# Nine columns instead of ten in the per-block list of edges outside the grid

## The chip, the cores and the metric

The kernel runs on one core of a Trainium2 chip. The metric is the device time of one execution in microseconds (us). TensorE is PE in the tables, VectorE DVE, ScalarE ACT, GpSimd POOL and SyncE SP.

## What is computed

Four graph layers run one after the other on 6,250 nodes with 64 features and 206,250 directed edges, sorted by destination. Each layer adds its result to x and normalizes. Cut to what matters (`w1`, `w2` are edge weights, `ea` the 32 features of an edge):

```
edges: 100000 random (s, d), both ways, and 6250 loops; sorted by dst
layer 0: relu(segment_sum(w1 * (x @ W_low)[src], dst)), the same with w2, W_high; attention of three branches
layer 1: segment_sum / max / mean(ea, by src) -> 2-layer MLP
layer 2: sum over k of segment_sum(gw_k(deg[src], deg[dst]) * (x @ g)_k[src], dst) / deg
layer 3: segment_sum(relu(W1 @ [x[src], x[dst], ea]) @ W2.T, dst) -> GRU cell
after each: x = layernorm(x + layer)
```

## The kernel before

The edges are cut into `NBK` = 51 blocks of `BE` = 4,096, read as 32 chunks of 128. Since they are sorted by destination, the destinations of a block lie within some 128 neighbouring nodes. A block has two stores in DRAM. One is a **grid** with one cell for each source node (49 x 128 cells): an edge may lie there if, counting chunk by chunk up to and with its own, it is the only edge of the block with its source, and its destination is under 128 above the block's first. All other edges go into the **list** of the block, in order. The list is cut into pieces of `SR = P * SC` slots, with `SC` columns of 128; a block has room for `NR` = 4 such pieces, and slots with no edge hold a fill row (source 6250, destination 6272, weights 0).

`placing` (L223) counts, decides for each edge, and scatters the rows. It ends with the number of rounds, from the longest list (`k.n_sec`, in slots):

```
incl[0] = max over blocks of n_sec
rounds  = 1 + (incl[0] > SR) + (incl[0] > 2 * SR) + (incl[0] > 3 * SR)     # L558 to L566
```

`k.counts_i[0]` holds it, `n_rounds` (L597) loads it into a register of each engine, and it is the count of the outer loop of `over_rounds` (L570) and `over_triples` (L583), each of which runs over all 51 blocks for every round:

```
with eng.Fori(0, rounds) as r:
    with eng.Fori(0, thirds // 2) as i: ...body(n, m, b, j, r)
```

Four stages run in this loop, and each round works on piece `r` of every block's list:

- **layer-0 sums** (`layer0_rest`, L613): POOL gathers the source rows of a piece, one indirect DMA for each column (L672), DVE weighs them and builds one-hot masks (L729, L741, L743), PE sums into 160 destinations (L704) and counts degrees (L708, three columns at a time). SP loads the pieces and, in the same body, writes zeros and far marks for later stages (L654, L655). The grid's part of layer 0 was done in `placing`.
- **layer-1 scatter** (`layer1_scatter`, L1012): sorts the list's rows by source; POOL scatters one column with each indirect DMA (L1091), to places from DVE (L1207); DVE ranks within a column (L1183).
- **layer-2 edges** (`layer2_edges`, L1638): each body does the grid (294 matmuls at L1712, masks at L1761) and the piece of the list (gathers at L1692, matmuls at L1725).
- **layer-3 edges** (`layer3_edges`, L2020): again the grid (L2145, L2149, L2163, L2166) and the piece (two gathers for a column, L2113 and L2116; masks L2307, matmuls L2214).

In the second and later rounds of layers 2 and 3 the grid's relative destinations come from the far marks (-128), so that its masks are all zero, but its instructions are the same. A block takes one of three buffers (`j`), semaphores set the order, and each engine follows its own stream. The order around the change is as written; nothing plans it.

Of the kernel before, what the change touches and what calls it, by code (L numbers as in the profile page):

```python
# [4 lines left out]
P = 128  # L5
CB = 32
BE = P * CB
SC = 10
SR = P * SC
NR = 4  # L10
SUB = 7
D = 64
F = 32
# [14 lines left out]
ACT = mybir.ActivationFunctionType  # L28
# [51 lines left out]
def make(nc, ctx):  # L80
    def sb(name, shape, dt=fp32):
        return ctx.enter_context(nc.sbuf_tensor(name, shape, dt))

    def ps(name, shape, dt=fp32):
        return ctx.enter_context(nc.psum_tensor(name, shape, dt))

    def sem(name):
        return nc.alloc_semaphore(name)

    return sb, ps, sem  # L90
# [132 lines left out]
def placing(nc, z, k, a):  # L223
    NT, NBK, HC = z.NT, z.NBK, CB // 2
    BK = 8
    with ExitStack() as ctx:
# [48 lines left out]
        gv = a["pay_d"][0:z.grid_rows, :].rearrange("(b l s) w -> b l (s w)", l=P, s=NT)  # L275
        sv = a["pay_d"][z.grid_rows:z.grid_rows + z.sec_rows, :].rearrange("(b p r) w -> b p (r w)", p=P, r=NR * SC)
        fg = a["fill"][0:z.cells, :].rearrange("(l s) w -> l (s w)", l=P)
# [292 lines left out]
def over_rounds(eng, z, k, body):  # L570
    thirds = z.NBK // 3
    rounds = n_rounds(eng, k)
    with eng.Fori(0, rounds) as r:
        with eng.Fori(0, thirds // 2) as i:
            for h in range(2):
                for j in range(3):
                    body(r * z.NBK + i * 6 + (h * 3 + j), r * thirds + i * 2 + h, i * 6 + (h * 3 + j), j, r)
        for m in range(thirds - thirds % 2, thirds):
            for j in range(3):
                body(r * z.NBK + (m * 3 + j), r * thirds + m, m * 3 + j, j, r)  # L580
# [28 lines left out]
def sec_view(z, a):  # L609
    return a["pay_d"][z.grid_rows:z.grid_rows + z.sec_rows, :].rearrange("(k p c) w -> k p (c w)", p=P, c=SC)  # L610


def layer0_rest(nc, z, k, a):  # L613
    NBK = z.NBK
    with ExitStack() as ctx:
        sb, ps, sem = make(nc, ctx)
        row = [sb(f"r0_row{j}", [P, SC, RW]) for j in range(3)]
        xs = [sb(f"r0_x{j}", [P, SC, D]) for j in range(3)]
        val = [sb(f"r0_val{j}", [P, SC, 2 * D]) for j in range(3)]
        onehot = [sb(f"r0_onehot{j}", [P, SC, WS]) for j in range(3)]  # L620
# [391 lines left out]
def layer1_scatter(nc, z, k, a):  # L1012
    NT = z.NT
    with ExitStack() as ctx:
# [11 lines left out]
        lo_hot = sb("s_lo_hot", [P, SC * P])  # L1026
# [8 lines left out]
        turned = ps("s_turned", [P, 2, 1024], bf16)  # L1035
# [11 lines left out]
        with nc.Block() as block:  # L1047
            @block.sync
            def _(sp):
                sp.wait_ge(nothing_set, 1)  # L1050

                pairs = scan_pairs(sp, z, k)

                def clear(j):
                    for q in range(4):
                        sp.dma_start(quarter(a["sorted_d"], z, pairs, q, j), nothing[:, :]).then_inc(cleared, 16)

                for j in range(3):
                    clear(j)
                with sp.Fori(0, pairs) as i:  # L1060
                    clear(i * 2 + 3)
                    clear(i * 2 + 4)

                def load(at_row, m, j):
                    sp.wait_ge(rows_out[j], m * (SC * 16) + 16)
                    sp.sem_inc(k.sync_steps, 1)
                    sp.dma_start(row[j][:, :, :].rearrange("p c w -> p (c w)"),
                                 sv[bass.ds(at_row, 1)].rearrange("k p w -> (k p) w")).then_inc(row_in[j], 16)

                def body(n, m, b, j, r):  # L1070
                    load(b * NR + r, m, j)

                over_rounds(sp, z, k, body)
                rounds = n_rounds(sp, k)
                load(0, rounds * (z.NBK // 3), 0)
# [24 lines left out]
            @block.scalar  # L1100
            def _(act):
                sc = nc.scalar

                def spread(n, j):
                    act.wait_ge(keys_ready, n + 1)
                    sc.activation(keys[:, :, :], key[j][:, :].unsqueeze(2).to_broadcast([P, SC, P]), ACT.Copy).then_inc(bc_in, 1)

                def copies(n):
                    act.wait_ge(turned_ready, n + 1)
                    sc.activation(lo_hot[:, 0:8 * P], turned[:, 0, :], ACT.Copy).then_inc(lo_hot_ready, 1)  # L1110
                    sc.activation(lo_hot[:, 8 * P:SC * P], turned[:, 1, 0:2 * P], ACT.Copy).then_inc(lo_hot_ready, 1)

                def body(n, m, b, j, r):
                    spread(n + 1, (j + 1) % 3)
                    copies(n + 1)

                spread(0, 0)
                copies(0)
                over_rounds(act, z, k, body)
# [900 lines left out]
def layer3_edges(nc, z, k, a):  # L2020
# [6 lines left out]
    with ExitStack() as ctx:  # L2027
# [16 lines left out]
        ea_s = sb("m_ea_s", [P, 3 * P])  # L2044
# [7 lines left out]
        pre_s = ps("m_pre_s", [P, 2, 512])  # L2052
# [13 lines left out]
        with nc.Block() as block:  # L2066
# [154 lines left out]
            @block.scalar  # L2221
            def _(act):
                sc = nc.scalar

                def copies(n, u):
                    act.wait_ge(turned, n * NS + (u + 1))
                    act.wait_ge(pre_ready, n * NS + (u + NS))
                    sc.activation(ea_t[u % 2][:, 0:P], ea_ps[u % 2][:, 0:P], ACT.Copy).then_inc(copied, 1)
                    sc.activation(ea_t[u % 2][0:SB * F, P:2 * P], ea_ps[u % 2][0:SB * F, P:2 * P], ACT.Copy).then_inc(copied, 1)  # L2229

                def high(n, u):
                    act.wait_ge(added, n * NS + (u + 3))
                    act.wait_ge(hid_used, n * NS + (u + (NS - 1 if u < LAG else NS + 2 - RING)))
                    sc.activation(parts[u % RING][:, :, 0:D], hid[u % 3][:, :].rearrange("p (s d) -> p s d", d=D), ACT.Relu).then_inc(hi_ready, 1)

                def middle(n, u):
                    act.wait_ge(left_ready, n * NS + (u + 1))
                    sc.activation(parts[u % RING][:, :, D:2 * D], left[u % RING][:, :].rearrange("p (s d) -> p s d", d=D), ACT.Copy).then_inc(mid_ready, 1)

                def keep(n, j):  # L2240
                    act.wait_ge(grid_in, n * 16 + 16)
                    sc.activation(ea[j][:, :].rearrange("p (s f) -> p s f", f=F), grid[:, :, 0:F], ACT.Copy).then_inc(kept, 1)

                act.sem_inc(copied, 3)
                act.sem_inc(kept, 1)
                keep(0, 0)

                def body(n, m, b, j, r):
                    copies(n, 0)
                    for u in range(NS):  # L2250
                        if u + 1 < NS:
                            copies(n, u + 1)
                        if u == 1:
                            act.wait_ge(row_in[j], m * 16 + 16)
                            act.wait_ge(pre_s_ready, n + 1)
                            sc.activation(ea_row[:, :].rearrange("p (c f) -> p c f", f=F), row[j][:, :, 0:F], ACT.Copy).then_inc(row_kept, 1)
                        if u == 6:
                            keep(n + 1, (j + 1) % 3)
                        if u == 3:
                            act.wait_ge(turned_s, n + 1)  # L2260
                            sc.activation(ea_s[:, 0:2 * P], pre_s[:, 0, 0:2 * P], ACT.Copy).then_inc(copied_s, 1)
                            sc.activation(ea_s[0:2 * F, 2 * P:3 * P], pre_s[0:2 * F, 0, 2 * P:3 * P], ACT.Copy).then_inc(copied_s, 1)
                        if u == 5:
                            act.wait_ge(added_s, n + 2)
                            sc.activation(hid_s[:, :], hid_s[:, :], ACT.Relu).then_inc(hid_s_ready, 1)
                        high(n, u)
                        if u:
                            middle(n, u - 1)
                    middle(n, NS - 1)

                over_rounds(act, z, k, body)

            @block.vector
# [391 lines left out]
```

## Time and profile before

| | us |
|---|---|
| median of 3 runs | 9233.94 |
| lowest and highest | 9219.14, 9248.25 |
| profiled execution, first to last instruction | 9369.1 |
| PE, DVE, POOL busy | 5537.1, 5345.0, 4789.4 |
| mean granted TensorE clock | 0.731 |

The profiled execution is the one that the rows below show. Its span is 1.5% over the median of the timed runs; no separate time is given for it beside the span. No engine is busy for more than 60% of the span, so the stages have to be read apart.

### The profile page before, as it was taken

Reading aid. Unit: us, or ns where it says so; the run is one execution under the profiler, and the core shown is the slowest. Engines: PE = TensorE matmul, PEld = TensorE weight load, DVE = VectorE, ACT = ScalarE, POOL = GpSimd, SP = SyncE. Lnnn points to the kernel's source line nnn. Section 1 sums busy time; section 2 is a strip of 40 time slices with the busy share of each in tenths; the row PEclk is TensorE's granted clock in tenths of the full one; section 3 lists DMA queues with packets and bytes.
Section 4 is the critical chain, followed back from the end, with each engine's and each line's share of the span. In section 5 each row is a group of like instructions: output and inputs, shape, how many; then the busy total and the mean of one; then the engine's idle time right before and its main releaser. Section 6 shows DMA issues by size and latency. Waiting matters only on the chain. (4 is left out here: it accounts for less than half of the span.)

```text
span 9369.1 us, 138875 instructions
## 1 busy us (share of the span) xinstructions
PE 5537.1 (59%) x49076; PEld 4542.6 (48%) x49077; DVE 5345.0 (57%) x9166; ACT 1663.2 (18%) x3235; POOL 4789.4 (51%) x4394
## 2 busy tenths in 40 slices
PE   2555555555555523233455542899996677777777
PEld 1333333333333322223345441899995566666665
DVE  5555655565556533334344455666665677777773
ACT  0111111111111100002111131000002333333333
POOL 3555555555555454550355551455550577667670
PEclk7666676666666666665666675999996788888885
DMA  3222222221222154441100030111110333333330
GB/s 98 77 82 78 73 75 81 78 78 70 81 78 80 40 92 89 88 88 29 42 20 19 20 109 12 26 26 27 27 27 17 106 100 97 95 93 95 95 92 13
DMA packets 392774, 612.74 MB, mean 65 GB/s; under 512 B 158383, under 2 KB 318995, under 8 KB 377363
## 3 DMA queue, kind: packets, MB, share of 16 engines
q1 hardware_dynamic: 240826, 478.03, 16.7%
q0 software_dynamic: 141056, 124.52, 6.4%
q8 instruction: 313, 5.13, 0.2%
q10 hardware_dynamic: 10454, 4.04, 0.2%
q14 instruction: 125, 1.02, 0.0%
HBM read 531.52 MB, written 216.25 MB: 80 GB/s over the span
## 5 line engine op out<-in xcount | busy, mean ns | idle before, releaser
L321 POOL DMA_INDIRECT pay_d<-row,place x1632 | 1719.7, 1054 | 1524.9 <-DVE place L497 947.9
L415 PE MATMUL win<-onehot,val 128*128 128x128 f32 x4998 | 1045.4, 353 | 672.4 <-issue 455.3
L415 PEld LDWEIGHTS win<-onehot,val 128*128 128x128 f32 x4998 | 872.3, 251 | 926.8 <-issue 644.4
L514 DVE TENSOR_TENSOR onehot<-near_dve,drel 128x896 f32<-128x896 f32 x357 | 389.3, 1091 | 1182.2 <-remote 1057.4
L2113 POOL DMA_INDIRECT m_from_src<-from_src_d,m_row x510 | 684.0, 1341 | 628.5 <-issue 375.4
L1712 PE MATMUL g_win<-g_hot,y_part 128*128 128x128 bf16 x14994 | 880.7, 220 | 145.1 <-DVE g_hot L1761 101.1
L1692 POOL DMA_INDIRECT g_x<-xg_d,g_row x510 | 641.5, 1258 | 625.1 <-PE g_win L1712 411.7
L1712 PEld LDWEIGHTS g_win<-g_hot,y_part 128*128 128x128 bf16 x14994 | 857.3, 99 | 166.8 <-DVE g_hot L1761 102.1
L1091 POOL DMA_INDIRECT sorted_d<-s_row,s_place x510 | 494.1, 969 | 531.0 <-DVE s_place L1207 368.5
L672 POOL DMA_INDIRECT r_x<-in_x,r_row x510 | 485.2, 951 | 500.9 <-DMA r_row<-pay_d 351.2
L2116 POOL DMA_INDIRECT m_from_dst<-from_dst_d,m_row x510 | 631.0, 1237 | 160.0 <-issue 155.7
L390 PE MATMUL pair<-hot_hi,hot_lo 128*128 128x392 bf16 (+3 forms) x1632 | 295.5, 346 | 639.2 <-DVE hot_hi L453 627.6
L337 ACT ACTIVATE hot<-onehot 128x896 bf16<-128x896 f32 x357 | 333.7, 950 | 1728.3 <-DVEq L521 1720.9
L390 PEld LDWEIGHTS pair<-hot_hi,hot_lo 128*128 128x128 bf16 x1632 | 197.3, 127 | 765.4 <-DVE hot_hi L453 375.8
L704 PE MATMUL r_win<-r_onehot,r_val 128*128 128x160 f32 x1020 | 231.6, 395 | 558.7 <-DVEq L731 369.0
L2145 PE MATMUL m_pre<-m_w_four,m_ea_t 96*128 96x192 f32 (+1 forms) x1428 | 487.4, 425 | 117.1 <-ACT m_ea_t L2229 93.1
L704 PEld LDWEIGHTS r_win<-r_onehot,r_val 128*128 128x128 f32 x1020 | 210.6, 265 | 582.7 <-DVEq L731 394.5
L2149 PEld LDWEIGHTS m_pre<-m_q_win,m_hot_t 128*128 128x128 bf16 x7497 | 360.4, 104 | 202.5 <-issue 135.1
L2149 PE MATMUL m_pre<-m_q_win,m_hot_t 128*128 128x64 bf16 x7497 | 395.8, 201 | 96.3 <-issue 94.2
L2285 DVE TENSOR_TENSOR m_hot<-iota,m_drel 128x896 bf16<-128x896 f32 x361 | 391.8, 1086 | 87.8 <-DMA xt<-in_xT 70.8
L2163 PE MATMUL m_win<-m_hot,m_parts 128*128 128x128 bf16 x2499 | 356.2, 232 | 111.9 <-issue 111.3
L1761 DVE TENSOR_TENSOR g_hot<-iota,g_drel 128x896 bf16<-128x896 f32 x364 | 375.0, 1087 | 82.0 <-PE g_win L1712 55.5
(410 smaller groups left out, 11491.4 us busy)
## 6 DMA issues: line engine op xcount, KB each, us to landing
m_hot_t<-drow_d SPq DMA_DIRECT2D x52, 1568.0 KB
scan_d<-in_none SPq DMA_DIRECT2D x51, 1034.2 KB
lo_row<-lo_d SPq DMA_DIRECT2D x51, 1024.0 KB
m_grid<-pay_d SPq DMA_DIRECT2D x52, 882.0 KB
pay_d<-in_fill SPq DMA_DIRECT2D x51, 882.0 KB
grid<-pay_d SPq DMA_DIRECT2D x51, 882.0 KB, 3.8
pay_d<-in_fill SPq DMA_DIRECT2D x51, 720.0 KB
row<-in_pay SPq DMA_DIRECT2D x51, 576.0 KB
```

What stands on the lines that cost most here:

```text
L321: pool.indirect_dma_start(a["pay_d"][:, :], bass.IndirectOffsetOnAxis(ap=place[j][:, c:c + 1], axis=0), row[j][:, c, :], None).then_inc(ro ...
L390: last = mm(pair[h][:, q, c * NT:BK * NT].rearrange("p (n s) -> p n s", s=NT), hot_lo[:, e, :], hot_hi[:, e, :].unsqueeze(1).to_broadcast( ...
L415: mm(win[:, :], val[u % 2][:, s, :], onehot[u % 2][:, s, :], start=(u == 0 and s == 0), stop=(u == NS - 1 and s == SUB - 1))
L672: pool.indirect_dma_start(xs[j][:, c, :], None, a["x"][:, :], bass.IndirectOffsetOnAxis(ap=row[j][:, c, AT_SRC:AT_SRC + 1].bitcast(i32), a ...
L704: mm(win[j][:, :], val[j][:, c, :], onehot[j][:, c, :], start=(c == 0), stop=(c == SC - 1))
L1091: pool.indirect_dma_start(a["sorted_d"][:, :], bass.IndirectOffsetOnAxis(ap=place[j][:, c:c + 1], axis=0), row[j][:, c, :], None).then_inc ...
L1692: pool.indirect_dma_start(xs[j][:, c, :], None, a["xg_d"][:, :], bass.IndirectOffsetOnAxis(ap=row[j][:, c, AT_SRC:AT_SRC + 1].bitcast(i32) ...
L1712: last = mm(win[:, h, 0:W], k.y[q][:, t, h * P:(h + 1) * P], hot[u][:, s, :], start=(t == 0 and q == 0), stop=(t == NT - 1 and q == 2))
L2113: pool.indirect_dma_start(ps_x[j][:, c, :], None, a["from_src_d"][:, :], bass.IndirectOffsetOnAxis(ap=row[j][:, c, AT_SRC:AT_SRC + 1].bitc ...
L2116: pool.indirect_dma_start(qs_x[j][:, c, :], None, a["from_dst_d"][:, :], bass.IndirectOffsetOnAxis(ap=row[j][:, c, AT_DST:AT_DST + 1].bitc ...
L2145: mm(out[:, first * D:(first + size) * D], ea_t[u % 2][0:size * F, o:o + P], w_four[0:size * F, 0:size * D], start=True, stop=False)
L2149: last = mm(out[:, s * D:(s + 1) * D], hot_t[j][:, (u * SUB + s) * P:(u * SUB + s + 1) * P], q_win[j][:, q * D:(q + 1) * D], start=False, ...
```

## The change

`SC` goes from 10 to 9. Every loop over columns then has nine turns, a piece has `SR` = 1,152 slots where it had 1,280, and two written-out sizes follow `SC`.

```
@@ -5,7 +5,7 @@
-SC = 10
+SC = 9
 SR = P * SC
@@ -1108,7 +1108,7 @@ def copies(n):
-                    sc.activation(lo_hot[:, 8 * P:SC * P], turned[:, 1, 0:2 * P], ACT.Copy).then_inc(lo_hot_ready, 1)
+                    sc.activation(lo_hot[:, 8 * P:SC * P], turned[:, 1, 0:(SC - 8) * P], ACT.Copy).then_inc(lo_hot_ready, 1)
@@ -2259,7 +2259,7 @@ if u == 3:
-                            sc.activation(ea_s[0:2 * F, 2 * P:3 * P], pre_s[0:2 * F, 0, 2 * P:3 * P], ACT.Copy).then_inc(copied_s, 1)
+                            sc.activation(ea_s[0:(SC - 8) * F, 2 * P:3 * P], pre_s[0:(SC - 8) * F, 0, 2 * P:3 * P], ACT.Copy).then_inc(copied_s, 1)
```

On POOL, in the layer-0 sums, these are the gathers of the loop over rounds; L574 is the inner loop over blocks, L573 the loop over rounds, L669 the wait for a piece:

```order
 L574 ISA
-L672 DMA r_x<-in_x,r_row 128x64 x30
+L672 DMA r_x<-in_x,r_row 128x64 x27
 L669 ISA
-L672 DMA r_x<-in_x,r_row 128x64 x30
+L672 DMA r_x<-in_x,r_row 128x64 x27
 L574 REGISTER_ALU
 L574 COMPARE_AND_BRANCH
 L669 ISA
-L672 DMA r_x<-in_x,r_row 128x64 x30
+L672 DMA r_x<-in_x,r_row 128x64 x27
 L573 REGISTER_ALU
 L573 COMPARE_AND_BRANCH
```

Three blocks have 27 gathers where they had 30; the branch of L573 still closes the loop, and its count is a register's.

On PE, in the same stage, this is one block of the loop (L704 sums messages, L708 counts degrees):

```order
 L700 ISA
 L702 ISA
-L704 MATMUL r_win<-r_onehot,r_val 128x160 x10
+L704 MATMUL r_win<-r_onehot,r_val 128x160 x9
 L705 ISA
 L708 MATMUL r_deg_ps<-r_hot,r_ones 1x480 x3
-L708 MATMUL r_deg_ps<-r_hot,r_ones 1x160
 L700 REGISTER_ALU
 L700 COMPARE_AND_BRANCH
```

One matmul of ten is gone, and one of the four that count degrees, since nine columns are three whole groups of three.

## Rows read from the trace of the kernel before

**Rows 1.** The page: span, and busy time of each engine.
```profile
span 9369.1 us, 138875 instructions
PE 5537.1 (59%) x49076; PEld 4542.6 (48%) x49077; DVE 5345.0 (57%) x9166; ACT 1663.2 (18%) x3235; POOL 4789.4 (51%) x4394
```
**Rows 2.** Busy time by stage: stretch, length, engines, then clock, DMA share, GB/s.
```profile
3297.00:4276.00 979.00, 289.10 (x1224) 224.50 (x1224) 360.67 (x613) 78.38 (x51) 485.21 (x510) 0.61 0.48 86
4495.00:5456.00 961.00, 512.80 (x3100) 461.83 (x3100) 423.27 (x1812) 132.34 (x156) 494.09 (x510) 0.66 0.08 20
5871.00:7076.00 1205.00, 1155.65 (x17085) 1134.21 (x17085) 800.12 (x1078) 13.78 (x51) 641.46 (x510) 0.98 0.14 27
7290.00:9183.00 1893.00, 1425.83 (x16116) 1165.34 (x16116) 1391.12 (x2046) 675.54 (x1684) 1315.01 (x1020) 0.86 0.31 95
```
**Rows 3.** The page's groups: indirect DMAs on POOL in the four stages.
```profile
L2113 POOL DMA_INDIRECT m_from_src<-from_src_d,m_row x510 | 684.0, 1341 | 628.5 <-issue 375.4
L1692 POOL DMA_INDIRECT g_x<-xg_d,g_row x510 | 641.5, 1258 | 625.1 <-PE g_win L1712 411.7
L1091 POOL DMA_INDIRECT sorted_d<-s_row,s_place x510 | 494.1, 969 | 531.0 <-DVE s_place L1207 368.5
L672 POOL DMA_INDIRECT r_x<-in_x,r_row x510 | 485.2, 951 | 500.9 <-DMA r_row<-pay_d 351.2
L2116 POOL DMA_INDIRECT m_from_dst<-from_dst_d,m_row x510 | 631.0, 1237 | 160.0 <-issue 155.7
```
**Rows 4.** Timeline, layer-0 sums: start, duration, instruction, idle before it.
```profile
3621.31 0.95 POOL L672 DMA_INDIRECT r_x<-in_x,r_row  x1 [20.07 <-DMA r_row<-pay_d]
...
3657.76 0.95 POOL L672 DMA_INDIRECT r_x<-in_x,r_row  x1 [0.30 <-issue]
3659.62 0.29 PE L708 MATMUL r_deg_ps<-r_hot,r_ones 128*1 128x160 bf16 x1 [2.23 <-issue]
3663.99 0.33 DVE L755 TENSOR_TENSOR acc<-r_win,acc 128x160 f32 x1 [28.35 <-remote]
3665.26 1.80 DVE L729 TENSOR_TENSOR r_onehot<-r_near_dve,r_rel 128x1600 f32<-128x1600 f32 x1
...
3678.82 0.95 POOL L672 DMA_INDIRECT r_x<-in_x,r_row  x1 [20.11 <-DMA r_row<-pay_d]
```
**Rows 5.** Timeline, layer-1 scatter.
```profile
4869.91 0.97 POOL L1091 DMA_INDIRECT sorted_d<-s_row,s_place  x1 [14.49 <-DVE s_place L1207]
4911.79 0.97 POOL L1091 DMA_INDIRECT sorted_d<-s_row,s_place  x1 [0.30 <-issue]
4913.06 0.35 DVE L1183 SCALAR_TENSOR_TENSOR s_junk<-key_bc,s_key,before 128x128 bf16<-128x128 f32 x1 [15.78 <-remote]
4925.20 0.97 POOL L1091 DMA_INDIRECT sorted_d<-s_row,s_place  x1 [12.44 <-DVE s_place L1207]
```
**Rows 6.** Layer-2 edges: two stretches, late blocks on DVE, the list's matmuls.
```profile
5870.00:6110.00 240.00, 219.37 (x3165) 213.16 (x3166) 150.83 (x203) 2.43 (x9) 126.73 (x104) 0.94 0.15 28
6830.00:7076.00 246.00, 239.19 (x3581) 235.81 (x3579) 169.24 (x227) 2.97 (x11) 125.24 (x98) 1.00 0.14 24
7011.72 0.17 DVE L1772 CAST g_dst_f<-g_row 128x10 f32<-128x10 int32 x1 [2.03 <-issue]
7055.89 0.17 DVE L1772 CAST g_dst_f<-g_row 128x10 f32<-128x10 int32 x1 [1.69 <-issue]
L1725 PE MATMUL g_win_s<-g_onehot,g_val 128*128 128x160 f32 x2040 | 290.0, 302 | 0.0
```
**Rows 7.** Layer-3 edges by line (min/median/max ns, first to last start); list's matmuls.
```profile
L2313 DVE CAST m_dst_f<-m_row x51: 158/166/168, 7316.6 to 9156.7; 128x10 f32<-128x10 int32 x51
L2113 POOL DMA_INDIRECT m_from_src<-from_src_d,m_row x510: 938/1226/3377, 7297.7 to 9150.8; - x170
L2214 PE MATMUL m_win_s<-m_onehot,m_hid_s 128*64 128x160 f32 x1020 | 193.6, 357 | 0.8 <-issue 0.5
```
**Rows 8.** Timeline, last block: last gather, sum that reads it.
```profile
9152.01 0.94 POOL L2116 DMA_INDIRECT m_from_dst<-from_dst_d,m_row  x1 [0.30 <-issue]
9164.60 0.82 DVE L2322 TENSOR_TENSOR m_from_src<-m_from_src,m_from_dst 128x640 f32<-128x640 f32 x1
```

## Prediction

> **What bounds the kernel now.** I read the page first: on a span of 9369.1 us no engine is busy for over 59% [rows 1], so no single engine sets the time. I then took busy time by stage [rows 2]. Each of the four stages that loop over rounds has x510 gathers or scatters on POOL (x1020 in layer 3, two for a column), which is 51 blocks x 10 columns x **one** round. The four stages last 979, 961, 1205 and 1893 us, together 5038 us, over half of the span. `placing` comes before them, takes about a third of the span, and has no loop over rounds.
>
> Inside the stages I read timelines. In the layer-0 sums, POOL issues 30 gathers for three blocks without a break, one every 1.26 us (0.95 and 0.30 idle), and then stands for 20.1 us until a piece is loaded; the bursts start 57.5 us apart [rows 4]. While POOL bursts, PE's matmuls come one by one, with idle of 2.2 us before them that no semaphore explains, and DVE stands for 28.35 us; DVE goes on 5.3 us after the last gather is over, so the three blocks last burst + 20 us. The scatter has the same form: DVE resumes 0.3 us after the last of POOL's column DMAs, and three blocks take 4925.20 - 4869.91 = 55.3 us, of which 30 x (0.97 + 0.30) = 38.1 are POOL's [rows 5]. Layer 2 is PE's: it is busy for 1155.65 of 1205 us [rows 2]; early in the stage the granted clock is 0.94, late 1.00, and two late blocks take 7055.89 - 7011.72 = 44.2 us, 22.1 each, against a mean of 1205 / 51 = 23.6 [rows 6]. Layer 3 is mixed: (9156.7 - 7316.6) / 50 = 36.8 us a block [rows 7], of which POOL takes 20 gathers x (1.29 + 0.30) = 31.8 us, the mean of its two gathers being 1.29 [rows 3], so that little is left in which POOL waits.
>
> **The change, first part: how many rounds.** The trace does not show the longest list, only that it is at most 1,280 slots. It follows from the edges. I drew them as the reference does and counted by the kernel's rule: in a block, chunk by chunk, an edge goes to the list unless the count of its source up to and with its chunk is one and its destination is under 128 above the block's first. The last block has 2,646 padded edges, which the kernel subtracts. The 51 lists have a mean near 1,110; the longest has **1,179** slots. Seven of them are over 1,152: blocks 15, 21, 22, 23, 32, 33 and 35, with 1,158, 1,174, 1,162, 1,179, 1,170, 1,155 and 1,157. They are over by 6 + 22 + 10 + 27 + 18 + 3 + 5 = 91 edges. With SR = 1,280 the formula gives 1 + 0 = 1 round, with SR = 1,152 it gives 1 + 1 = **2 rounds**. Every engine runs the body of all 51 blocks a second time in four stages, for 91 edges. The count of a round is fixed by the code, not by how full a piece is, so the second round's pieces, nearly all fill rows, cost DMAs and matmuls like the first. Nothing else hides this: the stages follow one another, and each ends when its last round does.
>
> **Second part: what a block saves with nine columns.** Per stage, before and after:
>
> - *Layer-0 sums.* Three blocks have three gathers fewer: 3 x 1.26 = 3.8 us off the burst. In the 20 us behind it DVE does about three masks (1.80 us for ten columns [rows 4], 0.18 a column each) and a little more, 0.7 us in all. Triple: 57.5 - 3.8 - 0.7 = 53.0; a round of 17 triples: 901 us, against 977.5. Two rounds: 1802, **+824**. The zeros and far marks that SP writes are written twice too; they are inside the body.
> - *Scatter.* 3 x 1.27 = 3.8 us off the burst; in the gaps (17 us in all, the larger 12.4 [rows 5]) ranks, masks and PE's products have a tenth less, 1.3 us by my reckoning. 55.3 - 5.1 = 50.2; a round 853 against 940. Two rounds: 1707, **+767**.
> - *Layer 2.* A block has 4 of 40 list matmul records fewer: 290.0 / 510 = 0.57 us for each column [rows 6]. First round 23.6 - 0.6 = 23.0 x 51 = 1174 us. The second starts where the first ended, at clock 1.00: 22.1 - 0.6 = 21.5 x 51 = 1097. Together 2271 against 1205: **+1066**.
> - *Layer 3.* Two gathers fewer: 2 x 1.59 = 3.2 us of POOL. PE saves 193.6 / 510 = 0.4 us, DVE two masks' tenth. POOL and PE share the pace, so the saving lies between 0.6 (only the cheaper DVE and PE work counts) and 3.8 us (all of it, with POOL's in full); nearer to neither, I take 2.0: 34.8 us a block, 1775 for 51, and the 16 us of start and end (1893 - 51 x 36.8) once. Two rounds: 3566 against 1893: **+1673**.
> - *Everywhere else*: `placing` fills 128 x 4 slots less for a block, by DMAs that SP issues long before they are needed; its POOL and DVE work is the same, so I take nothing. The copies of ACT and the turned tails are a tenth of small work under other engines. The outer branch costs one turn more for each engine and stage: nothing.
>
> Sum: 824 + 767 + 1066 + 1673 = +4330; 9369 + 4330 = 13,699 us of span. The timed median is 9234 / 9369 = 0.986 of the profiled span, and I scale by that: **13,500 us**.
>
> A rule of the Trainium skill bears on the bursts. The rows show PE's matmuls 2.2 us apart with no semaphore behind it while POOL issues DMAs, and it ends with the burst [rows 4]; by this the burst's 3.8 us are saved in full. "Runtime: NRT & Kernel Launch", section Instruction fetch mechanics, says that a taken branch whose target is outside the small window of instructions forces a DMA fetch before execution goes on. By that rule the stall would hang on the branches and on the DMA traffic (unchanged, from SP's writes), not on POOL's count, and a triple would be 57.5 - 0.7 = 56.8 us: 129 us more over two rounds of the layer-0 sums. The trace has no record of a fetch by which to decide; that the stall's end keeps to the burst's end speaks for the first.
>
> **Bounds.** The unknown is how much of POOL's shorter burst each stage keeps. None of it: triples of 56.8 and 54.0 us (+129 each over 34 triples), layer 3 at 36.2 (+143 over 102 blocks), and layer 2's second round at the first's 23.0 (+76): +477, 14,176 us of span, 13,970 timed. All of it: layer 3 at 33.0 (-184), another 1 us off each triple of the two earlier stages (-68), layer 2's late blocks at 21.0 (-26): 13,421, or 13,230 timed. If the profile's surplus is a constant 135 us and no ratio, the centre is 13,560.
>
> **The rivals.**
>
> 1. *Two rounds, at the price above.* 0.87.
> 2. *One round.* The other side: the change doesn't do this, if the longest list is not over 1,152 slots. It decides at exactly one slot past 1,152, and seven blocks are past it, not one. For it speaks only that the count is my own and the trace holds none. It would save one round's part: 76 + 87 + 31 + 102 = 296 us, 9073 of span, 8,940 timed. 0.05.
> 3. *Two rounds, the second dearer.* In the second round nearly all gathers read one and the same row of DRAM. If that slows each gather of layer 3 to the 3.4 us that the longest takes now [rows 7], it alone adds (3.4 - 1.29) x 18 x 51 = 1.9 ms: near 15,400. Against it: the last block has 182 real slots, so most of its gathers read the fill row already; its last gather takes 0.94 us, and the sum that reads it has no wait, 11.7 us after the gather's end [rows 8]. 0.04.
> 4. *Two rounds at the old price or cheap ones.* If nine columns save nothing: 9369 + 5038 = 14,407, 14,200 timed; if the second round's zeros let it run far quicker than the first, below 13,100. Nothing in the rows points to a price by values. 0.04.
>
> **How the numbers follow.** The forecast is that of the first case, 13,500. Its bounds, 13,230 and 13,970, widened a little below, give 13,150 to 13,950; the other cases hold 0.13 and lie far off, so the range need not reach them. A measurement of this kernel can tell 0.3% from no change (28 us); no case lies near it. Faster 0.05, same 0.01 (a cancellation that no case describes), slower 0.94.
>
> **What would show it.** In the profile after: L672, L1091 and L1692 x918 (51 x 9 x 2), L2113 and L2116 x918 each; L1712 x29988; stages of about 1800, 1710, 2270 and 3570 us; bursts of 27 gathers, 53 us apart; the granted clock at 1.00 through layer 2's second round. If these counts are 459, the second rival holds. If they are 918 and the stages are longer, the second half of each stage against its first tells whether fill rows are dearer; if both halves are equally long, the columns saved less than I took.

## The result

The changed kernel takes **13667.72 us** (median of 4 runs, 13642.65 to 13697.89) beside 9226.54 us for the kernel before (4 runs): a ratio of 1.4799, 95% interval 1.4773 to 1.4825. It is 48% slower. Forecast were 13,500 us, a ratio of 1.462.

The page of the kernel after: span, busy time by engine, then the granted clock and the DMA share in 40 slices, the gathers' DMA queue, and the groups that answer to [rows 3].

```profile
span 13680.5 us, 235116 instructions
PE 8524.8 (62%) x85027; PEld 7279.1 (53%) x85028; DVE 8078.1 (59%) x14468; ACT 2515.2 (18%) x5173; POOL 7077.0 (52%) x6434
...
PEclk7666666666665655666675999999789889988886
DMA  2222222222459992000020111333133333444442
...
q0 software_dynamic: 206336, 186.48, 15.3%
...
L1712 PE MATMUL g_win<-g_hot,y_part 128*128 128x128 bf16 x29988 | 1739.3, 220 | 162.1 <-DVE g_hot L1761 100.7
...
L1692 POOL DMA_INDIRECT g_x<-xg_d,g_row x918 | 1162.8, 1267 | 1194.5 <-PE g_win L1712 881.7
L2113 POOL DMA_INDIRECT m_from_src<-from_src_d,m_row x918 | 1163.5, 1267 | 1161.6 <-PE m_pre L2149 557.0
...
L672 POOL DMA_INDIRECT r_x<-in_x,r_row x918 | 876.2, 954 | 1030.0 <-DMA r_row<-pay_d 762.5
...
L1091 POOL DMA_INDIRECT sorted_d<-s_row,s_place x918 | 891.6, 971 | 828.5 <-DVE s_place L1207 525.6
...
L2116 POOL DMA_INDIRECT m_from_dst<-from_dst_d,m_row x918 | 1125.6, 1226 | 279.9 <-issue 256.1
```

The counts are those of two rounds of nine columns: 918 = 51 x 9 x 2 for each gather and scatter, 29988 = 2 x 14994 for the grid's matmuls. No engine is much nearer to being full than it was in [rows 1] (PE 62% after 59%, DVE 59% after 57%, POOL 52% after 51%); there is mainly more of the same. Busy time of the four stages, each cut where its second round begins (columns as in [rows 2]):

```profile
3284.00:4133.00 849.00, 250.55 (x1071) 207.73 (x1071) 335.94 (x613) 71.55 (x51) 457.98 (x480) 0.61 0.54 100
4133.00:5167.00 1034.00, 284.62 (x1071) 239.82 (x1071) 337.75 (x607) 71.53 (x51) 418.19 (x439) 0.60 0.92 75
5391.00:6205.00 814.00, 429.95 (x2736) 398.11 (x2736) 384.68 (x1676) 118.60 (x153) 430.33 (x443) 0.68 0.08 21
6205.00:7047.00 842.00, 444.78 (x2808) 412.98 (x2808) 395.80 (x1716) 120.73 (x156) 461.30 (x475) 0.68 0.08 21
7461.00:8623.00 1162.00, 1122.08 (x16935) 1106.83 (x16936) 768.17 (x1079) 13.83 (x51) 592.59 (x469) 0.99 0.14 26
8623.00:9759.00 1136.00, 1108.11 (x16830) 1096.42 (x16827) 760.67 (x1071) 13.83 (x51) 570.21 (x450) 0.99 0.35 25
9979.00:11733.00 1754.00, 1359.67 (x16100) 1125.73 (x16101) 1367.08 (x2053) 674.44 (x1696) 1183.26 (x938) 0.90 0.33 102
11733.00:13495.00 1762.00, 1375.11 (x15929) 1133.04 (x15927) 1355.57 (x2034) 666.99 (x1671) 1105.79 (x899) 0.89 0.48 95
```

Every first round is shorter than its stage in [rows 2] (in part because this profile comes from a quicker chip, see below), and a second one follows it. One pair stands out: in the layer-0 sums the second round takes 1034 us after a first of 849, with the same instructions and PE's clock unchanged, while the DMA share (the time of all packets, as a share of the 16 engines' time) goes from 0.54 to 0.92 and the rate of the bytes moved falls from 100 to 75 GB/s. What DVE, POOL and SP wait for in 700 us of each of these two rounds (first stretch 3400 to 4100, second 4300 to 5000; total, times, longest):

```profile
DVE acc L755 <- remote: 236.0, 24, 22.1
POOL r_x L672 <- DMA r_row<-pay_d: 217.3, 20, 16.2
SPq L651 <- DVEq L746: 426.3, 37, 27.1
...
DVE r_val L741 <- DMA r_x<-in_x,r_row: 331.7, 28, 19.6
POOL r_x L672 <- DMA r_row<-pay_d: 307.4, 20, 28.7
SPq L651 <- DVEq L746: 22.3, 10, 9.9
```

In the first round DVE waits for PE's window (the wait of L755; the view names no releaser but "remote"), as before, and never for a gather's data. In the second it is the data that come late. So do the pieces that POOL waits for: SP, which loads them, waited 426 us for free buffers in the first round and 22 us in the second, so that buffers are there and its loads are behind all the same. The last block of layer 3, as in [rows 8], and the late blocks of the first stage's second round, as in [rows 4]:

```profile
4710.89 0.95 POOL L672 DMA_INDIRECT r_x<-in_x,r_row  x1 [28.66 <-DMA r_row<-pay_d]
...
4737.88 0.76 DVE L741 TENSOR_TENSOR r_val<-r_x,r_near_dve 128x576 f32<-128x576 f32 x1 [18.85 <-DMA r_x<-in_x,r_row]
...
4761.73 0.95 POOL L672 DMA_INDIRECT r_x<-in_x,r_row  x1 [17.20 <-DMA r_row<-pay_d]
...
13460.19 0.96 POOL L2116 DMA_INDIRECT m_from_dst<-from_dst_d,m_row  x1 [0.30 <-issue]
...
13476.49 0.75 DVE L2322 TENSOR_TENSOR m_from_src<-m_from_src,m_from_dst 128x576 f32<-128x576 f32 x1
```

Layer 3's last sum still finds its data there, 15 us after the gather's end.

The experiments ran on other chips, on which the kernel before takes 9375 us (experiments 1 to 4), 9363 us (5 to 7 and 9) and 9372 us (8). Its profile ahead of the prediction, with a span of 9369.1, is alike to those, so times per block are compared with that profile and with the changed kernel's run on such a chip (below), and total times by their ratios to the kernel before on the same chip. Experiments 3 and 5 ran on two of these chips, so their difference in total time is less certain than what the two rounds of one profile show. "Per block" is the spacing of DVE's first instruction of a block (L735, L1167, L1772, L2313), mean over the 50 spacings of a round.

### The profile page after: what moved, and what is told of

Its sections match the earlier page's. It is cut to its first block and busy times, and to the rows that moved or that the text cites. A ratio compares the mean times of both kernels' runs of the same rounds, so it can differ in the third digit from the quotient of the medians.

```text
span 13680.5 us, 235116 instructions
## 1 busy us (share of the span) xinstructions
PE 8524.8 (62%) x85027; PEld 7279.1 (53%) x85028; DVE 8078.1 (59%) x14468; ACT 2515.2 (18%) x5173; POOL 7077.0 (52%) x6434
## 3 DMA queue, kind: packets, MB, share of 16 engines
q0 software_dynamic: 206336, 186.48, 15.3%
## 5 line engine op out<-in xcount | busy, mean ns | idle before, releaser
L1712 PE MATMUL g_win<-g_hot,y_part 128*128 128x128 bf16 x29988 | 1739.3, 220 | 162.1 <-DVE g_hot L1761 100.7
L1712 PEld LDWEIGHTS g_win<-g_hot,y_part 128*128 128x128 bf16 x29988 | 1708.8, 98 | 188.1 <-DVE g_hot L1761 100.9
L1692 POOL DMA_INDIRECT g_x<-xg_d,g_row x918 | 1162.8, 1267 | 1194.5 <-PE g_win L1712 881.7
L2113 POOL DMA_INDIRECT m_from_src<-from_src_d,m_row x918 | 1163.5, 1267 | 1161.6 <-PE m_pre L2149 557.0
L672 POOL DMA_INDIRECT r_x<-in_x,r_row x918 | 876.2, 954 | 1030.0 <-DMA r_row<-pay_d 762.5
L1091 POOL DMA_INDIRECT sorted_d<-s_row,s_place x918 | 891.6, 971 | 828.5 <-DVE s_place L1207 525.6
L704 PE MATMUL r_win<-r_onehot,r_val 128*128 128x160 f32 x1836 | 459.8, 435 | 1356.7 <-DVEq L731 1071.6
L2116 POOL DMA_INDIRECT m_from_dst<-from_dst_d,m_row x918 | 1125.6, 1226 | 279.9 <-issue 256.1
L704 PEld LDWEIGHTS r_win<-r_onehot,r_val 128*128 128x128 f32 x1836 | 429.7, 299 | 1405.4 <-DVEq L731 1103.5
L2145 PE MATMUL m_pre<-m_w_four,m_ea_t 128*128 128x256 f32 (+1 forms) x2856 | 959.4, 420 | 138.1 <-ACT m_ea_t L2229 119.8
L2163 PE MATMUL m_win<-m_hot,m_parts 128*128 128x128 bf16 x4998 | 708.4, 233 | 222.2 <-issue 222.0
L2166 PE MATMUL m_win<-m_hot,m_parts 128*128 128x128 bf16 x4998 | 690.7, 232 | 184.1 <-DVE m_parts L2303 154.4
L2291 DVE TENSOR_TENSOR m_hid<-m_pre,pq 128x448 f32<-128x448 f32 x714 | 444.0, 622 | 596.0 <-remote 297.8
```

What stands on the lines that cost most here:

```text
L672: pool.indirect_dma_start(xs[j][:, c, :], None, a["x"][:, :], bass.IndirectOffsetOnAxis(ap=row[j][:, c, AT_SRC:AT_SRC + 1].bitcast(i32), a ...
L704: mm(win[j][:, :], val[j][:, c, :], onehot[j][:, c, :], start=(c == 0), stop=(c == SC - 1))
L1091: pool.indirect_dma_start(a["sorted_d"][:, :], bass.IndirectOffsetOnAxis(ap=place[j][:, c:c + 1], axis=0), row[j][:, c, :], None).then_inc ...
L1692: pool.indirect_dma_start(xs[j][:, c, :], None, a["xg_d"][:, :], bass.IndirectOffsetOnAxis(ap=row[j][:, c, AT_SRC:AT_SRC + 1].bitcast(i32) ...
L1712: last = mm(win[:, h, 0:W], k.y[q][:, t, h * P:(h + 1) * P], hot[u][:, s, :], start=(t == 0 and q == 0), stop=(t == NT - 1 and q == 2))
L2113: pool.indirect_dma_start(ps_x[j][:, c, :], None, a["from_src_d"][:, :], bass.IndirectOffsetOnAxis(ap=row[j][:, c, AT_SRC:AT_SRC + 1].bitc ...
```

## The experiments

**Theory.** The count of rounds is the whole loss: 91 edges over 1,152 slots make every engine run four stages twice. Nine columns by themselves save. A second, small part: reads of one fill row make the second round of the layer-0 sums dearer. **Rival:** the second round costs what it does for another reason (SP's clears, repeated in it, or the columns' own price), or nine columns are dearer in themselves.

**1. One round, 91 edges left out.** `k.counts_i` is a constant 1; the edges past slot 1,152 of seven blocks are left out.

```
-   v.tensor_copy(k.counts_i[:, 0:1], incl[0:1, NR - 1:NR])
+   v.tensor_scalar(k.counts_i[:, 0:1], incl[0:1, NR - 1:NR], 0.0, 1.0, ALU.mult, ALU.add)
```

> Nine columns with the number of rounds set to the constant 1; the 91 edges past slot 1,152 are left out. Theory (the whole loss is the second round): faster than before. The trace of the change has first rounds of 16.4, 16.0, 22.6 and 33.7 us a block in the four stages against 19.2, 18.4, 23.5 and 36.8, which is 51 x (2.8 + 2.4 + 0.9 + 3.1) = 470 us: 9227 - 470 = 8,760 us. By the savings of the prediction (296 us) it would be 8,930. Rival (nine columns themselves are dearer, by the sizes of pieces or of the copies): 9,230 us or more.

Measured: 9055.8 us, ratio 0.966 (0.9644 to 0.9677). Faster than before, so the sign of the result is the second round's alone. The saving that I expected, 470 us, was too high by 150: it came from times per block of two traces that were taken on two chips (below, in what was new). On the chip of the first result the ratio stands for 9227 x 0.966 = 8,913 us, where I had written 8,760. On one chip nine columns save 319 us; the prediction's second rival had it at 296.

**2. Ten columns, two rounds.** The kernel before with its count fixed at 2; nothing is left out.

> Ten columns as before, the number of rounds set to the constant 2; nothing is left out, the second round finds only fill rows. Theory: the second round costs what a first one costs, and more in the layer-0 sums: about 51 x (21.5 + 18.4 + 22.9 + 37.8) = 5,130 us more than before, near 14,350 us. Rival (a round is cheap unless it has real edges, and the change's loss came from the seven blocks with 91 edges): under 10,000 us. Second rival (the change's loss has a part that comes from nine columns): under 13,700 us.

Measured: 14602.96 us, ratio 1.5579 (1.5553 to 1.5605), of which 9227 x 1.5579 = 14,375 is the same on the chip of the first result; the first theory had 14,350. The second round of ten columns costs 5228 us, where the four stages of [rows 2] hold 5038. Per block, layer 0 takes 19.3 us in the first round and 22.1 in the second: the dearer second round does not come from nine columns. Layers 2 and 3 are dearer in their second round too, by 0.9 us a block each (23.4 and 24.2, 36.6 and 37.5); with nine columns layer 2 shows no such surplus (22.6 and 22.5 below), and no run says why.

**3 and 4. Fill rows spread.** The fill rows read sources 6250 to 6271 in turn and not 6250 alone, and in the fourth also destinations 6272 to 6399. Their weights stay 0.

```
-                       np.full(most, n, np.int32)),
+                       (n + np.arange(most) % (z.NP - n)).astype(np.int32)),
```

> The changed kernel, with the fill rows' source running over the 22 padded rows 6250 to 6271 in place of 6250 alone. Theory (in the second round nearly all gathers read one row of DRAM, and that is why a block of the layer-0 sums takes 20.4 us there against 16.4): the second round of the layer-0 sums comes near 16.4 us a block, 200 us less, and layer 3 gains up to 50: 13,420 to 13,470 us. Rival (the second round's repeated clears, or its place in time, make it slow): within 20 us of 13,670 us.

> As e3_fill_sources_spread, and the fill rows' destination runs over 6272 to 6399 in place of 6272 alone, so that the second gather of layer 3 is spread over 128 rows too. Theory: layer 3's second round, 34.7 us a block against 33.7 in the first, loses what e3_fill_sources_spread leaves of that 1 us: up to 50 us below e3_fill_sources_spread. Rival (layer 3's surplus isn't from the rows read): the same as e3_fill_sources_spread within 20 us.

**5. The changed kernel again**, as reference on such a chip.

> The changed kernel as it is, beside the next three kernels. The four earlier experiments ran on a chip on which the kernel before takes 9375 us, where it took 9227 us beside the changed kernel. If a slower chip scales every kernel alike, the ratio is 1.480 again, within 0.003, and the 1.1% by which the spread fill sources came out lower (1.4639 against 1.4799) is theirs. If chips differ in what slows one-row reads, the ratio is nearer 1.464 on a slow chip and the spread is worth nothing there.

Measured: spread sources 13721.82 us, ratio 1.4639 (1.4614 to 1.4663); both spread 13701.71 us, 1.4623 (1.4598 to 1.4647), which the intervals don't part from it; the changed kernel again 13921.88 us, 1.4857 (1.4826 to 1.4889). That last is neither of the two outcomes that I had named for it: it lies above 1.480 too. So the spread is worth 1.5%, some 200 us, against this run, and 1.1%, some 150 us, against the first result, where the theory had 200 to 250 and the rival under 20; what chips differ in is mixed into either figure. Windows of the second round of the layer-0 sums, of the changed kernel run again and then of the third experiment; of the latter also the gathers' DMA queue on its page, and what DVE waits for from 4300 to 5000:

```profile
4175.00:5267.00 1092.00, 283.28 (x1071) 237.96 (x1071) 343.38 (x617) 71.53 (x51) 421.29 (x442) 0.60 0.92 72
```
```profile
4180.00:5030.00 850.00, 231.61 (x1008) 191.92 (x1008) 324.10 (x592) 67.34 (x48) 418.25 (x439) 0.60 0.47 90
```
```profile
q0 software_dynamic: 206336, 186.48, 7.8%
```
```profile
DVE acc L755 <- remote: 312.9, 13, 25.4
```

The gathers move the same packets and bytes (206336, 186.48 MB), and their share of the DMA engines over the whole kernel falls from 15.3% to 7.8%. DVE is back at waiting for PE and never for a gather. A block of the second round goes from 21.3 to 16.9 us: 51 x 4.4 = 225 us, the whole of the gain. The first rounds of the two runs are alike, 17.2 and 17.4 us, so this is hardly a difference of chips. In layer 2 the share falls too, from 0.35 in the windows above to 0.13, and the time hardly does (22.5 and 22.4 us a block); layer 3's second round, 35.4 us a block, stays. With the destinations spread too it takes 35.1, 16 us over 51 blocks, which the totals can't tell from noise.

**6. Clears written once.** SP's zeros and far marks (L654, L655) leave the loop over rounds and follow it in a loop of their own over 51 blocks.

```
-                    sp.dma_start(zv[at(b)], a["none"], max_dma_last_dim=1024).then_inc(cleared, 16)
-                    sp.dma_start(dv[at(b)], a["far"]).then_inc(cleared, 16)
...
+                with sp.Fori(0, NBK) as b:
+                    sp.dma_start(zv[at(b)], a["none"], max_dma_last_dim=1024).then_inc(cleared, 16)
+                    sp.dma_start(dv[at(b)], a["far"]).then_inc(cleared, 16)
```

> The changed kernel, with SP's zeros and far marks written in a loop of their own over 51 blocks after the loop over rounds, once and not once for each round. Theory one: POOL's burst sets the pace of the layer-0 sums; the blocks stay at 16.4 us in the first round and 20.4 in the second, and the clears, now without cover, lengthen the stage by up to some 300 us. Theory two: the stall of PE and DVE and the dearer second round hang on the traffic of SP's clears; both rounds fall by 2 us a block or more (over 200 us for 102 blocks), which pays for the clears, and the ratio stays at 1.48 or falls. In between: the second round alone falls to the first's 16.4, 200 us, since one-row reads are dear only beside the clears.

Measured: 13962.53 us, ratio 1.4905 (1.4876 to 1.4935). The sum hides the finding, which is in the windows: first round, second round, and the clears by themselves.

```profile
3298.00:4186.00 888.00, 249.71 (x1071) 204.65 (x1071) 331.11 (x604) 71.55 (x51) 458.62 (x482) 0.61 0.17 28
4186.00:4960.00 774.00, 226.28 (x967) 186.16 (x968) 309.86 (x564) 65.94 (x47) 391.52 (x412) 0.61 0.81 28
4975.00:5335.00 360.00, 35.14 (x161) 32.81 (x161) 25.25 (x45) 4.21 (x3) 12.01 (x13) 0.52 1.06 161
```

The first round keeps its 17.3 us a block (17.2 with the clears), and the second falls from 21.3 to 16.2: the expectation's case in between. With the clears gone, the second round still holds the DMA engines for 0.81, where the first holds them for 0.17 at the same 28 GB/s, and it costs no time; it is even 1.1 us a block quicker than the first, which no run explains. The gathers' queue in 700 us of each of these two rounds (3450 to 4150, 4250 to 4950; packets, MB, share):

```profile
q0 software_dynamic: 11925, 12.23, 10.7%
...
q0 software_dynamic: 12158, 12.47, 78.6%
```

The packets are as many and as large, and take seven times as long. Beside the clears (0.54 - 0.17 = 0.37 in the first round) that is more than the engines have, and the sums agree: a block of one-row gathers and pieces needs 0.81 x 16.2 = 13.1 us of all engines, its clears 0.37 x 17.2 = 6.4, together 19.5, and the changed kernel's second round shows 0.92 x 21.3 = 19.6. That is when data come late. From DVE's last block of this stage to its first of the scatter it is now 530 us, where it was 240 (the last window above holds the clears and three late blocks): 290 us of clears without cover, which take back the 261 us.

**7. Even blocks: nine columns that fit.** Each block gets `z.BR` = 4,045 real edges (the last 4,000) and fills up at its own end, where 50 blocks held 4,096 and the last held 1,450; all edges are computed. Core of the edit (the host's arrays are laid out so, and the padded edges are taken off each block's count):

```
+    z.BR = -(-e // blocks)
...
+                v.tensor_scalar(k.n_sec[:, :], k.n_sec[:, :], float(z.BR - BE), None, ALU.add)
...
+        array = rows(array, NBK_ * z.BR, fill).reshape(NBK_, z.BR)
+        tail = array[:, -1:] if last else np.full((1, 1), fill, array.dtype)
+        return np.ascontiguousarray(np.concatenate([array, np.broadcast_to(tail, (NBK_, BE - z.BR))], axis=1)).reshape(-1)
```

> Nine columns, and the edges dealt to the 51 blocks evenly: 4,045 real edges in each block with the fill at its own end, where now 50 blocks hold 4,096 and the last holds 1,450. By my count the longest list then has 1,151 slots, one under the limit, so that one round does it with no edge left out. If the count of rounds is the whole loss, this is the nine-column kernel at one round: ratio 0.966, and x459 gathers at the first gather line. If the count is wrong by two slots, it goes to two rounds and 1.47. If dealing evenly costs something of its own in the phases before, it lies above 0.966 by that.

Measured: 9031.38 us, ratio 0.9635 (0.9611 to 0.9659), as expected and within noise of the first experiment's 0.966, here with every edge computed. The count shows the one round:

```profile
L2116 POOL DMA_INDIRECT m_from_src<-from_src_d,m_row x459 | 566.3, 1234 | 758.3 <-issue 362.0
...
L675 POOL DMA_INDIRECT r_x<-in_x,r_row x459 | 436.5, 951 | 440.8 <-DMA r_row<-pay_d 307.0
```

**8. Even blocks, ten columns**, the control for the dealing.

> Edges dealt evenly as in the nine-column kernel of even blocks, but ten columns as before; one round in either. It is the control for the dealing. If the dealing itself costs and brings nothing, it lies within 0.3% of the kernel before, and the whole gain of 3.5% is the columns'. If the last block, now as full as the others, or the shorter chunks change something, it shows here; each block has 51 edges fewer, so that the longest list is shorter, but no loop follows that length: 0.996 to 1.004.

Measured: 9383.46 us, ratio 1.0011 (0.9996 to 1.0025). The dealing itself changes nothing that can be measured; the 3.65% of the seventh experiment are the column's.

**9. Even blocks, nine columns, the tenth gather put back** in the layer-0 sums and (both gathers) in layer 3. It repeats column 8 into a column that nothing reads.

```
-                    for c in range(SC):
+                    for c in range(SC + 1):
+                        d = min(c, SC - 1)
```

> The evenly dealt nine-column kernel, with a tenth gather for each block in the layer-0 sums and a tenth pair in layer 3, which read column 8 once more into a column that nothing uses; all other work stays that of nine columns. Theory one: the burst sets the pace of the layer-0 sums, and they lose 1.25 us a block, 64 us, and layer 3, where POOL and PE share the pace, 1.0 to 3.2 us a block, 50 to 160 us: 115 to 225 us over the kernel of even blocks, ratio 0.978 to 0.990. Theory two: the columns' saving lies in DVE's and PE's work, and the gathers were covered: within 0.3% of the kernel of even blocks.

Measured: 9187.11 us, ratio 0.981 (0.9791 to 0.983), 156 us over the seventh. Nine columns save 331 us in all, in four stages; nearly half of it comes back with the gathers of these two, with no DVE or PE work in it. (Each gather also moves its 128 rows. The run doesn't part that from POOL's time, but in layer 0, from 3400 to 4100, DVE waits for no gather's data.) By stage, DVE's first instruction of a block in layer 0 and layer 3, of the seventh kernel and of this one:

```profile
L738 DVE CAST r_dst_f<-r_row x51: 173/174/405, 3294.5 to 4147.0; 128x9 f32<-128x9 int32 x51
...
L2316 DVE CAST m_dst_f<-m_row x51: 159/166/168, 7065.1 to 8820.2; 128x9 f32<-128x9 int32 x51
```
```profile
L739 DVE CAST r_dst_f<-r_row x51: 173/173/393, 3300.7 to 4210.2; 128x9 f32<-128x9 int32 x51
...
L2318 DVE CAST m_dst_f<-m_row x51: 159/167/168, 7125.2 to 8959.5; 128x9 f32<-128x9 int32 x51
```

Layer 0: 852.5 / 50 = 17.05 against 909.5 / 50 = 18.19 us, +1.14 for one gather of 1.26 us. Layer 3: 35.10 against 36.69, +1.59 for two gathers of 3.2 us together.

## Why the prediction was right, and what was off in it

**The count of rounds: right.** 1,179 slots, seven blocks over, two rounds; x918 and x29988 in the page say two, and the seventh kernel, which fits by one slot of the same count (1,151), ran one. The second rival, one round, did not occur, but its price was good: 296 us forecast, 319 measured with the 91 edges left out. The fourth did not either: nine columns save, and the second round of the changed kernel is no cheaper than the first. Without the crowded DMA engines it would be, in layer 0, by little: 16.2 against 17.3 us a block in the sixth experiment, 16.9 against 17.4 in the third.

**The sizes.** Per block, in us, on chips alike to the one of the rows before (first and second round):

| stage | before | forecast | changed kernel again | over two rounds: forecast, measured |
|---|---|---|---|---|
| layer-0 sums | 19.2 | 17.7, 17.7 | 17.2, 21.3 | 1802, 1968 |
| scatter | 18.4 | 16.7, 16.7 | 16.1, 16.3 | 1707, 1691 |
| layer 2 | 23.5 | 23.0, 21.5 | 22.6, 22.5 | 2271, 2307 |
| layer 3 | 36.8 | 34.8, 34.8 | 35.0, 35.4 | 3566, 3613 |

The stages' lengths are from the first instruction to the last, with the same edges as in [rows 2]. Together 9579 against 9346: 233 us, and the span, 13925.9, is 227 over the 13,699 of the sum.

- *Layer-0 sums*, the term that was mis-sized: +824 forecast, 1968 - 979 = +989 measured. The step that failed was that the second round costs like the first. The first is 0.5 us a block cheaper than forecast, and the second 4.1 dearer than the first: 51 x 4.1 = 209 us, of which the cheaper blocks give back some 45 over both rounds. The third rival had the cause, reads of one row of DRAM, but looked for it in layer 3, by the length of a gather on POOL. That length did not move (L672 954 ns on average, 951 in [rows 3]); the price is paid in the DMA engines, and counts only where the clears fill them too. The evidence that I had against it, the last block of layer 3 [rows 8], was true and still is, but of another stage.
- *Scatter*: right within 1%. Its first round saves 2.3 us a block against my 1.7.
- *Layer 2*: the first round saves 0.9 and not 0.6. The second should have gained from the clock of 1.00 that [rows 6] show late in the stage. Both rounds ran at 0.99 in the changed kernel and at equal pace, 22.6 and 22.5: the second round's term was 1.0 us a block too low. What slows the first blocks in [rows 6] is not settled by a run.
- *Layer 3*: +1673 forecast, +1720 measured. I took 2.0 us of at most 3.8 (3.2 of POOL and 0.6 of DVE and PE); the first round kept 1.8. The ninth experiment splits it: 1.6 us are the two gathers', half of their 3.2.
- *"The burst's 3.8 us are saved in full"*: nearly. A tenth gather costs 1.14 of its 1.26 us. With SP's clears out of the first round (DMA share 0.54 to 0.17) a block took 17.3 us, as with them, and with a gather more, at the same branches, 1.14 more. So it is the count of gathers that sets the pace, and not the branches or the DMA traffic. I had also written that the trace has no record of a fetch. It has: the page of before lists queues for instructions, and the DMA view of 3450 to 4200, 750 us of the layer-0 sums with 13 bursts and their stalls, lists two queues and neither of these:

```profile
q8 instruction: 313, 5.13, 0.2%
...
q14 instruction: 125, 1.02, 0.0%
```
```profile
q1 hardware_dynamic: 60429, 51.85, 37.7%
q0 software_dynamic: 12480, 12.80, 10.0%
```

"Runtime: NRT & Kernel Launch", section Instruction fetch mechanics of the Trainium skill, has a taken branch outside the small window of instructions wait for a DMA fetch. No instructions were fetched in these 750 us, so that rule is not what stalls PE and DVE here. What does is open.

**The scaling by 0.986.** The number did its work by luck, for the reason was wrong. I took it for a surplus of a profiled execution over timed ones. There is none: the span of each profile of an experiment is within 0.2% of its runs' median. On three other chips the kernel before has medians of 9363 to 9375 us, and its profiled span, 9369.1, is alike to those; that it was taken on such a chip is my reading, since no record names its chip. The changed kernel was then timed on the quicker one. On a chip like the span's it takes 13,922 us, where the sum had 13,699. The alternative that I gave, a constant of 135 us, was wrong with it.

**The range** held the time. Its bounds came from the share of POOL's saving that a stage keeps; measured, that is between half (layer 3) and nine tenths (layer 0).

## What to carry to other kernels

A tile size that feeds a ceiling has to be judged by the largest count in the data, not by work saved per tile: one slot over the limit repeats all four stages of the loop, and here 91 edges of 206,250 make the kernel 4,441 us slower in all, while the column is worth 3.65% where the list fits. Before giving the column up, look whether the counts can be evened out; dealing the same edges in blocks of 4,045 instead of 4,096 brought the longest list from 1,179 to 1,151 and made the change a gain. It fits by one slot, for these edges: for others the loop over rounds still guards it, at the price above. And let padding entries of a gather point at different rows.

## What was not expected of the hardware

- **Gathers that read one row over and over hold the DMA engines about seven times as long**: 78.6% of their time against 10.7% for as many packets and bytes, in two rounds of one kernel (the sixth experiment), with POOL's 0.95 us for each issue unchanged. Spread over 22 rows, the load is gone. Beside other traffic (0.37) it delays the data. The pieces that SP loads come later as well: in 700 us of the changed kernel's second round POOL waits 307.4 us for them, at most 28.7 at a time, against 217.3 and 16.2 in its first round, and 253.4 and 19.2 in the second with the fill spread. "DMA: Bandwidth & Descriptors", section Queues, rings and completion order of the Trainium skill, says that each engine takes turns between its queues, a packet at a time; by this a slow packet of the gather holds up SP's too, which agrees with these waits, though no run here shows the turns themselves.
- **Chips differ by 1.6%, and not evenly over a kernel.** The kernel before takes 9227 us on one and 9363 to 9375 on three others. (Each was timed at one time only, so that a chip and its hour are not told apart.) The changed kernel's first rounds take 16.4 and 33.7 us a block in layers 0 and 3 on the first, 17.2 and 35.0 on another, but 16.0 and 16.1 in the scatter and 22.6 on both in layer 2. Times per block from two chips gave the first experiment's wrong 8,760 us.
- **A gather on POOL is time for others**: in layer 0 a gather that nothing needs costs 1.14 us of its 1.26, though PE is busy for 30% of the stage and DVE for 39%.
